# One attention and FFN layer on one core: SiLU, gate and maxima by pairs of tiles, and another order of work in the first batch

## The reference

```python
x = x + attn(cond(x, k, k, w1, u1, emb), w_qkv, b_qkv, w_out, b_out)
x = x + ffn(cond2(x, k, k, w2, u2, emb), W_up, W_gate, W_down)
# cond: bidirectional decaying scans of exp(k)*v and exp(k) over tokens, with an extra
#   exp(u+k) term, then sigmoid(x) * num / max(den, 1e-8) * gain
# attn: 16 heads of 16 channels, causal softmax, output projection
# ffn: W_* rounded to -1, 0, 1 times mean|W|;  hidden = silu(x Wup) * (x Wgate);  hidden Wdown
```

## Time and profile before

| what | value |
|---|---|
| three runs | 206.41, 207.51, 208.41 us; median 207.51 |
| profiled execution | 207.22 us |
| its span | 205.4 us (1.8 us lie around it) |
| DVE busy | 158.0 us, 77% |
| PE busy | 156.4 us, 76% |
| ACT busy | 116.4 us, 57% |
| POOL busy | 60.8 us, 30% |
| turn of batch 0 / 1 / 2 / 3 / tail | ends near 70 / 110 / 149 / 183 / 205 us |

### The profile page before, as it was taken

One profiled execution on the slowest core, in us unless ns is written; L12 is line 12 of the kernel. 1 busy time (PEld: TensorE's weight loads), 2 busy tenths in 40 slices (PEclk: granted clock), 3 DMA queues, 4 the chain that ended last, 5 costly groups with the idle time before them and its releaser, 6 DMA issues.

```text
span 205.4 us, 3560 instructions
## 1 busy us (share of the span) xinstructions
PE 156.4 (76%) x1436; PEld 99.1 (48%) x1436; DVE 158.0 (77%) x245; ACT 116.4 (57%) x181; POOL 60.8 (30%) x56
## 2 busy tenths in 40 slices
PE   0037929257989287968999589599996998997992
PEld 0037823002358155754567358355764684364681
DVE  0899995999895999999998899998239872315452
ACT  2739759417863931469568345775561459661450
POOL 8500529920200327843004192700104232000000
PEclk9999995555799979999999999879997999999998
DMA  4997130000002200000121000003200000100001
GB/s 112 397 428 314 51 104 0 3 0 2 0 3 78 77 0 3 0 2 3 60 98 51 0 3 1 2 7 110 93 0 0 0 6 0 54 0 0 3 0 51
DMA packets 5704, 10.88 MB, mean 53 GB/s; under 512 B 760, under 2 KB 4024, under 8 KB 5304
## 3 DMA queue, kind: packets, MB, share of 16 engines
q1 hardware_dynamic: 5400, 10.52, 13.4%
q10 hardware_dynamic: 288, 0.14, 0.4%
HBM read 6.43 MB, written 1.05 MB: 36 GB/s over the span
## 4 chain that ended last, share of the span: by engine, by line
DVE 41%; PE 36%; ACT 8%; issue 8%; DMA 3%; POOL 2%; POOLq 1%; DVEq 0%; ACTq 0%
PE attn_ps L923 10%; DVE row_max L588 8%; DVE fwd L521 7%; DVE bwd L531 7%; PE attn_ps L837 6%; PE wide L896 3%; PE wide L901 3%; PE turn_ps L806 3%; PE acc_ps L806 3%; DVE fwd L537 2%; PE acc_ps L850 2%; DMA k_t<-k_d 2%; PE acc_ps L934 2%; DVE hid L619 2%; POOL hid_lo L249 1%
## 5 line engine op out<-in xcount | busy, mean ns | idle before, releaser
L387 ACT ACTIVATE silu<-attn_ps,up_scale 128x256 f32<-128x256 f32 x32 | 15.2, 474 | 34.2 <-PE attn_ps L837 33.4
L588 DVE TENSOR_REDUCE row_max<-wide 128x4 f32<-128x1024 f32 (+1 forms) x24 | 28.8, 1217 | 2.4 <-PE wide L876 2.1
L369 ACT ACTIVATE probs<-wide 128x1024 f32<-128x1024 f32 x24 | 24.2, 1020 | 6.2 <-PE wide L901 5.8
L219 POOL TENSOR_TENSOR extra<-extra,k_t 128x512 f32<-128x512 f32 x7 | 9.4, 1346 | 61.3 <-DVE extra L506 61.3
L531 DVE TENSOR_TENSOR_SCAN bwd<-ek,decay 128x255 f32<-128x255 f32 x32 | 25.9, 857 | 0.0
L521 DVE TENSOR_TENSOR_SCAN fwd<-decay,ek 128x256 f32<-128x256 f32 x32 | 24.9, 820 | 0.1
L837 PE MATMUL attn_ps<-x_hi,w_tern 128*128 128x256 f16 x128 | 19.8, 278 | 4.7 <-DVE x_hi L605 3.2
L837 PE MATMUL attn_ps<-x_lo,w_tern 128*128 128x256 f16 x128 | 20.1, 282 | 3.4 <-DVE x_lo L611 3.4
L225 POOL TENSOR_TENSOR fwd<-fwd,extra 128x1024 f32<-128x1024 f32 x6 | 14.0, 2349 | 18.4 <-DVE x_lo L611 18.4
L619 DVE TENSOR_TENSOR hid<-silu,attn_ps 128x256 f32<-128x256 f32 x32 | 13.2, 416 | 7.0 <-ACT silu L387 7.0
L249 POOL TENSOR_TENSOR hid_lo<-hid,hid_hi 128x512 f16<-128x512 f32 x12 | 14.8, 1233 | 12.4 <-ACT hid_hi L394 12.1
(11 more groups left out here) (112 smaller groups left out, 304.1 us busy)
## 6 DMA issues: line engine op xcount, KB each, us to landing
stack<-halves SPq DMA_DIRECT2D x24, 128.0 KB, 2.1
w_raw<-wup_d SPq DMA_DIRECT2D x1, 1024.0 KB, 11.4
w_raw<-wgate_d SPq DMA_DIRECT2D x1, 1024.0 KB, 13.1
w_raw<-wdown_d SPq DMA_DIRECT2D x1, 1024.0 KB, 15.0
out_d<-x_t SPq DMA_DIRECT2D x4, 256.0 KB, 2.3
wqkv<-wqkv_d SPq DMA_DIRECT2D x1, 768.0 KB, 7.2
k_t<-k_d SPq DMA_DIRECT2D x1, 768.0 KB, 8.6
x_t<-x_d SPq DMA_DIRECT2D x1, 768.0 KB, 10.0
```

The costliest lines, as they stand in the source:

```text
L369: nc.scalar.activation(probs[:, j, :], flat(wide[j % 2][:, :, :]), ACT.Exp, scale=SOFTMAX_SCALE).then_inc(prob_done, 1)
L387: nc.scalar.activation(silu[:, e % 2], attn_ps[:, e % 2, 0:T], ACT.Silu, scale=up_scale[:, 0:1]).then_inc(silu_done, 1)
L588: nc.vector.tensor_reduce(out, src, AX.X, ALU.max).then_inc(max_done, 1)
```

## The change

- **Pairs.** `silu` holds two pairs. ACT's `silu_up(g)` reads both banks of `attn_ps` at once (128x512) after both tiles of pair g; `gate(g)` on DVE multiplies a pair at once. PE makes score tiles and up_gate tiles two by two, DVE takes maxima two by two. Products 2g and 2g + 1 wait for the gate of the whole pair g - 1. Both `down(0)` and `down(1)` now precede `up_gate(6)`.
- **Sums and POOL's list.** DVE adds c = 0 of the next batch before c = 1 of this one; POOL does the low half of pair 2 before `gate_first`; ACT takes the first exponentials before `first_reciprocal(0, b + 1)`.
- **Tail.** DVE's list is gate(g), low half(g), for g = 0 to 3; ACT's is silu(g), high half(g - 1).
- **Batch 0.** Scans, halves and extra products change places; POOL's `add_extra(1, 0)` and `sums(1, 0)` go to DVE, behind `first_gate(1)`; the bias product goes behind the maxima; nine full products (`keep_busy`, 3 + 6 x 1) stand among the scores and five ahead of the turned scores; the last `weigh` precedes the keys of batch 1; row reciprocals and `normalize` of batch 0 move ahead of the halves and of `forward(1, 1, 1)`; `project` also waits for the low queries.

The diff, with indentation shortened by four:

```diff
@@ line 108 of before @@
     gd_scale = sb("gd_scale", [P, 1])
-    silu = sb("silu", [P, 2, T])
+    silu = sb("silu", [P, 2, EG, T])
     hid = sb("hid", [P, 2, EG, T])
@@ line 227 of before @@
 
-        def sums(c, b):
-            pool.wait_ge(fwd_extra[c], b + 1)
-            pool.wait_ge(bwd_done[c], 4 * b + 4)
-            nc.gpsimd.tensor_tensor(fwd[c][:, :, :], fwd[c][:, :, :], bwd[c][:, :, :],
-                                    ALU.add).then_inc(sum_done[c], 1)
-
         def gate_first(b):
@@ line 275 of before @@
 
-        pool.wait_ge(wkv1_done, 1)
+        pool.wait_ge(hi_done[1], 1)
         extra_products(1, 0)
+        pool.wait_ge(hi_done[0], 1)
         values_of_keys(1)
+        pool.wait_ge(score_done, 1)
         extra_products(0, 1)
-        add_extra(1, 0)
-        sums(1, 0)
         for i in range(3):
@@ line 290 of before @@
             pool.wait_ge(x2lo_done, b)
-            add_extra(1, b)
             if more:
                 add_extra(0, b + 1)
+            add_extra(1, b)
             low_hidden(b - 1, 0)
@@ line 297 of before @@
             low_hidden(b - 1, 1)
+            low_hidden(b - 1, 2)
             if more:
                 gate_first(b + 1)
-            low_hidden(b - 1, 2)
             low_hidden(b - 1, 3)
@@ line 382 of before @@
 
-        def silu_up(b, e):
-            act.wait_ge(ug_done, ET * b + e + 1)
-            if e >= 2:
-                act.wait_ge(hid_done, ET * b + e - 1)
-            nc.scalar.activation(silu[:, e % 2], attn_ps[:, e % 2, 0:T], ACT.Silu,
+        def silu_up(b, g):
+            act.wait_ge(ug_done, ET * b + EG * (g + 1))
+            if g >= 2:
+                act.wait_ge(hid_done, NG * b + g - 1)
+            nc.scalar.activation(silu[:, g % 2], attn_ps[:, :, 0:T], ACT.Silu,
                                  scale=up_scale[:, 0:1]).then_inc(silu_done, 1)
@@ line 390 of before @@
         def high_hidden(b, g):
-            act.wait_ge(hid_done, ET * b + EG * (g + 1))
+            act.wait_ge(hid_done, NG * b + g + 1)
             if g >= 2:
@@ line 439 of before @@
             if b:
-                row_reciprocals(f)
+                if b > 1:
+                    row_reciprocals(f)
                 if b + 2 < B:
@@ line 447 of before @@
                 tanh_x1(f)
-                for e in range(ET):
-                    silu_up(f, e)
-                    if e % EG == 0 and e:
-                        high_hidden(f, e // EG - 1)
-                    if e == 5:
+                for g in range(NG):
+                    silu_up(f, g)
+                    if g:
+                        high_hidden(f, g - 1)
+                    if g == 2:
                         minus_maxima(b)
@@ line 456 of before @@
             else:
-                for i in range(3):
-                    scale_weights(i)
+                scale_weights(0)
                 key_exp(2)
+                scale_weights(1)
+                scale_weights(2)
                 ternary_weights(0)
@@ line 470 of before @@
                     exp_probs(0, j)
+                row_reciprocals(0)
                 high_halves(1, 1)
                 high_halves(1, 0)
-            if more and b:
-                first_reciprocal(0, b + 1)
             if b:
                 exp_probs(b, 0)
+                if more:
+                    first_reciprocal(0, b + 1)
                 first_reciprocal(1, b)
@@ line 613 of before @@
 
-        def gate(b, e):
-            dve.wait_ge(silu_done, ET * b + e + 1)
-            g = e // EG
-            if g >= 2 and e % EG == 0:
+        def gate(b, g):
+            dve.wait_ge(silu_done, NG * b + g + 1)
+            if g >= 2:
                 dve.wait_ge(hidlo_done, NG * b + g - 1)
-            nc.vector.tensor_tensor(hid[:, g % 2, e % EG], silu[:, e % 2], attn_ps[:, e % 2, T:2 * T],
+            nc.vector.tensor_tensor(hid[:, g % 2], silu[:, g % 2], attn_ps[:, :, T:2 * T],
                                     ALU.mult).then_inc(hid_done, 1)
@@ line 629 of before @@
             for half in (1, 0):
-                if half == 0 or b == 0:
-                    forward(0, b, half)
+                forward(0, b, half)
                 backward(0, b, half)
@@ line 680 of before @@
 
+        clamp_extra(1, 0)
+        clamp_keys(1)
         for half in (1, 0):
-            if half:
-                clamp_extra(1, 0)
-                clamp_keys(1)
             backward(1, 0, half)
-            low_halves(0, half)
+        low_halves(0, 1)
+        clamp_extra(0, 1)
+        low_halves(0, 0)
+        for half in (1, 0):
             forward(1, 0, half)
-        clamp_extra(0, 1)
 
@@ line 692 of before @@
             if b:
-                normalize(f)
+                if b > 1:
+                    normalize(f)
                 if more:
@@ line 703 of before @@
                 gate(f, 0)
+                maxima(b, 2)
+                maxima(b, 3)
                 gate(f, 1)
-                maxima(b, 2)
+                maxima(b, 4)
+                maxima(b, 5)
                 gate(f, 2)
-                maxima(b, 3)
-                gate(f, 3)
-                maxima(b, 4)
-                gate(f, 4)
-                maxima(b, 5)
-                sums(1, b)
-                gate(f, 5)
-                bound_denominator(1, b)
                 if more:
                     sums(0, b + 1)
-                gate(f, 6)
-                if more:
                     bound_denominator(0, b + 1)
-                gate(f, 7)
+                sums(1, b)
+                gate(f, 3)
+                bound_denominator(1, b)
             else:
@@ line 735 of before @@
                     maxima(0, j)
-                    if j == 0:
-                        forward(0, 1, 1)
+                    if j == 2:
+                        clamp_keys(2)
                 dve.wait_ge(bo_total, 1)
@@ line 740 of before @@
                                         ALU.add).then_inc(bo_done, 1)
+                first_gate(1)
+                dve.wait_ge(prod_done[1], 1)
+                dve.wait_ge(fwd_done[1], 4)
+                nc.vector.tensor_tensor(fwd[1][:, :, :], fwd[1][:, :, :], extra[1][:, :, :],
+                                        ALU.add).then_inc(fwd_extra[1], 1)
+                sums(1, 0)
                 bound_denominator(1, 0)
-                first_gate(1)
-                clamp_keys(2)
                 dve.wait_ge(scale_done, 4)
@@ line 756 of before @@
             second_wkv(b)
+            if not b:
+                normalize(0)
             if more:
@@ line 777 of before @@
         for g in range(NG):
-            for e in range(EG):
-                gate(f, EG * g + e)
-                if e == 0 and g:
-                    dve.wait_ge(hidhi_done, NG * f + g)
-                    if g >= 3:
-                        dve.wait_ge(down_done, NG * f + g - 2)
-                    nc.vector.tensor_tensor(hid_lo[:, (g - 1) % 2], hid[:, (g - 1) % 2], hid_hi[:, (g - 1) % 2],
-                                            ALU.subtract).then_inc(hidlo_done, 1)
-        dve.wait_ge(hidhi_done, NG * B)
-        dve.wait_ge(down_done, NG * f + 2)
-        nc.vector.tensor_tensor(hid_lo[:, 1], hid[:, 1], hid_hi[:, 1], ALU.subtract).then_inc(hidlo_done, 1)
+            gate(f, g)
+            dve.wait_ge(hidhi_done, NG * f + g + 1)
+            if g >= 2:
+                dve.wait_ge(down_done, NG * f + g - 1)
+            nc.vector.tensor_tensor(hid_lo[:, g % 2], hid[:, g % 2], hid_hi[:, g % 2],
+                                    ALU.subtract).then_inc(hidlo_done, 1)
         finish(f)
@@ line 829 of before @@
             if e >= 2:
-                pe.wait_ge(hid_done, ET * b + e - 1)
+                pe.wait_ge(hid_done, NG * b + e // EG)
             for x, half in enumerate((x2_hi, x2_lo)):
@@ line 910 of before @@
                 if b:
-                    pe.wait_ge(hid_done, ET * b)
+                    pe.wait_ge(hid_done, NG * b)
             pe.wait_ge(prob_done, NT * b + j + 1)
@@ line 931 of before @@
             pe.wait_ge(heads_t_done, b + 1)
+            if b + 1 < B:
+                pe.wait_ge(lo_done[0], b + 2)
             for et in range(CT):
@@ line 960 of before @@
                 scores(b, 2)
+                scores(b, 3)
                 up_gate(f, 2)
-                scores(b, 3)
                 up_gate(f, 3)
                 scores(b, 4)
+                scores(b, 5)
                 up_gate(f, 4)
-                scores(b, 5)
+                up_gate(f, 5)
                 down(f, 0)
-                up_gate(f, 5)
                 turn_maxima(b)
+                down(f, 1)
                 up_gate(f, 6)
-                down(f, 1)
                 up_gate(f, 7)
@@ line 978 of before @@
                                  stop=True).then_inc(abs_total, 1)
+                keep_busy(3, attn_ps[:, 1, :])
+                for j in range(NT):
+                    scores(0, j)
+                    keep_busy(1, attn_ps[:, 1, :])
```

(7 more changed lines are left out.)

## The result

| what | before | after |
|---|---|---|
| median of the runs | 207.44 us (206.41 to 208.41, 4 runs) | 223.97 us (223.40 to 226.16, 4 runs) |
| ratio | | 1.080, 95% interval 1.075 to 1.086 |
| profiled execution, its span | 207.22, 205.4 us | 223.43, 221.6 us |
| PE, DVE, ACT, POOL busy | 156.4, 158.0, 116.4, 60.8 us | 160.1, 158.0, 112.3, 55.5 us |
| granted clock of PE, mean | 0.914 | 0.938 |

A forecast was written before the change was run, and what follows sets the result against it. DVE and PE were each busy three quarters of the span, so their waits for each other counted. 1.8 + 1.25 + 2 x 2.9 + 2.2 + 6.5 = 17.5 us on 207.2 gave 224.7 us, range 217 to 229.

The forecast's parts named there:

- Batch 0, +1.8: First batch: 5 us won at the maxima are lost again by a late bound, half-clock PE and late `normalize`; +1.8 us.
- a clash of the moved clamp with POOL: Batch 0, after three maxima: the clamp of exponentials waits for one POOL instruction more, 2.1 + 0.3 us; at best 0.3.
- a sign of being wrong: Batch 0: the prediction called itself wrong if the residual starts before 74 us; it forecast 76.6 instead of 74.77.
- Clock in batch 1, +1.25: Start of batch 1's FFN: PE idles from 73.4 to 78.8 us, so three product groups run at half clock; +1.25 us.
- Batches 1 and 2, +2.9 each: FFN to `wkv1`: gates 3.4 us apart, a late last gate, then bound and scans alternating with POOL; +2.9 us per batch.
- full alternation: Batches 1 and 2: DVE's bound and scans and POOL's instructions take turns, one whole instruction each, 6.25 us in all.
- Batch 3, +2.2: Batch 3: later last silu, high half and table load move the first exponential from 171.59 to 174.2 us, PE returns 0.4; +2.2.
- Tail, +6.5: After batch 3: every step of a pair runs in a row, 4.45 us per turn; last step at 208.5 instead of 201.97.
- the first rival: Tail: PE's clock falls there too, one or two pairs at half clock adding 1.75 us each; 228 us, chance 0.22.
- The rival "faster": Whole kernel: the 5 us won in batch 0 reach the keys and wide instructions save fixed cost; 201.0 us, chance 0.05.

The follow-up runs named there:

- the bound moved: Changed kernel with the addition, sum and bound of c = 1 in batch 0 put back ahead of `first_gate(1)` on DVE: 220.95 us, ratio 1.058.
- the change run again: The changed kernel without any edit, measured again beside the later kernels: 224.21 us, ratio 1.076.
- The idle products: Changed kernel plus PE products nothing reads, 20 ahead of the FFN of batch 1, 5 and 10 in the tail: 222.54 us, ratio 1.065.
- the kernel with short low halves: Changed kernel with POOL's low halves of pairs 2 and 3 written for 8 of 256 tokens only: 221.6 us, too spread for a ratio.
- all three repairs: Changed kernel with last pair's products before `down(1)`, next gate before low half in the tail, batch 0's bound before `first_gate(1)`: 212.83 us, ratio 1.019.
- the last kernel: Kernel before with only the new batch 0, its bound ahead of `first_gate(1)`, plus 20 unread PE products before batch 1's FFN: 205.34 us, ratio 0.978.

## Why the prediction was right

The forecast was 224.7 us, the median 223.97; the chain was the predicted one, and "slower" had been given 0.92. Term by term:

- **Batch 0, +1.8, measured +1.2 in the traces and +1.4 by the run of this part alone.** The mechanism was right: bias product, two wide additions, bound at 53.7 (I had 54.9), ACT idle for 4.62 us. Two sizes were off and partly cancelled. I put 2.4 us on a clash of the moved clamp with POOL; it took 0.42, because it met the gap between two of POOL's instructions (34.56 to 35.08 us), which I had taken to have none. In exchange the first scores came about 1 us later, since PE made the first keys at half clock (3.30 us instead of 1.97), and the last exponential waited 2.62 us for scores (1.12 with the bound moved). The price was an upper bound taken as likeliest. In the twelve profiles with this order the clamp took 0.42 us four times and 1.28 to 1.46 us eight times. So it is partly luck that +1.2 came near +1.8: in the eight profiles with the bound behind `first_gate(1)` the residual starts anywhere from 73.5 to 78.7 us. In two of them, of this part alone (73.51) and of the change run again (73.63), it starts before 74, which I had named as a sign of being wrong. The mechanism holds even there, for ACT idles 5.12 and 5.21 us ahead of the bound; the size of the term is what depends on the execution.
- **Clock in batch 1, +1.25: exact.** The idle products took away just this from the stage. In the change run again it was 1.0.
- **Batches 1 and 2, +2.9 each, measured 2.57 and 2.55.** The loop was 3.42 us (forecast 3.4), the fourth gate 4.89 behind the third (4.8), bound and scans 5.7 us (6.25: 0.5 less than full alternation gives, and the kernel with short low halves, 3.85 us against 4.4 by alternation, is under it by the same 0.5). I had not seen that the sum ahead of the fourth gate meets a low half on POOL; it costs little here, since DVE waits for that gate anyway. 1.1 us came back ahead of batch 3, since the kernel before loses some clock there itself; I had not looked at its PE at 131 to 136 us (granted clock 0.66), after which its keys start 1.1 us behind `wkv1`.
- **Batch 3, +2.2, measured +1.4.** Same cause: before starts this FFN at half clock (granted clock 0.66 from 155 to 160 us), after does not. From the first maxima to `normalize` it is 28.81 us after, 27.39 before, and 26.45 in the kernel with the bound moved and single tiles, which keeps its clock there: against that the pairs cost 2.4, as forecast. 1.5 of it is the second down product in front.
- **Tail, +6.5, measured +8.3.** The turn was 4.55 us (4.45); without the clock the tail costs 6.85. The rest is the first rival, with one pair of products at half clock. It is in three of the six profiles that have this tail without idle products, and was given 0.22 for the whole. So here the forecast as it stands missed and the rival came in; the rival's time, 228, assumed nothing returned elsewhere.
- **The rival "faster"** had its deciding point right: the bound had to be there when ACT is free for it. Where it was made so, batch 0 became 3.4 us shorter, and with single tiles the kernel became 1% faster. The pairs could not be rescued by it, for even with all three repairs they are 7 us behind single tiles (212.83 against 205.86): 3.6 in the tail, 1.4, 1.4 and 0.9 in batches 1 to 3.

That the sum came within 1 us is partly luck, by errors of both signs: 3.1 us too much up to the end of batch 3 and 1.8 too little behind it.

## What to carry to other kernels

Taking two tiles in one instruction saves a fixed cost once, but turns two buffers into one: PE, ACT and DVE then work one after another, and the loop is the sum of their times. Compare that sum (3.42 us here) with the bound of the busiest engine (2.96) before merging. When a stage is made earlier, look for the next instruction in each in-order list that is now the late one (here one clamp of 0.43 us), and judge it by stages, for PE's clock moves its losses about between stages and executions.

## What the runs showed of the hardware

- Two executions of one kernel differ by 2.3 us at the end of batch 0 and by 0.3 at the end. PE's granted clock fell in other stages, and the wait of 2.62 us in the tail preceded a fall in the first and not in the second.
- The kernel before varied by 2 us from run to run, the one with only the new batch 0 by 4. In the last kernel 202.66 us went with a mean granted clock of 0.966, and 207.12 with 0.942.
- A clamp of 512 columns took 0.42 us or 1.28 to 1.46 us in the same place of the first batch, by where its start fell among POOL's instructions.
